# Layers and experts of a two-layer model in one block, with the first list's weights and rows prepared inside the layers' last turn

## The chip, the core and the metric

The kernel runs on one core of one Trainium2 chip, in one launch. The metric is the device time in microseconds. One execution is also profiled; its trace is what the prediction is worked out from.

## The reference, cut to what matters

The input is x of 2 x 2048 x 256. Layer 0 is a gated linear attention and a small per-feature network, layer 1 a selective scan (a state-space layer) and a mixture of experts. Each part takes a layer norm of x, scales and shifts it by a modulation vector, and adds its result to x with a gate. Only the last part matters closely here:

```python
k = int(EXPERT_CAPACITY * t / e)                   # 512 rows for each of 8 experts
scores = jnp.einsum('ntd,ed->nte', x, gate_w)
probs = jax.nn.softmax(scores, axis=-1)
g, m = jax.lax.top_k(probs.transpose(0, 2, 1), k)  # each expert chooses its rows
xin = x[batch_idx, m]
h = jnp.einsum('nekd,edf->nekf', xin, w1)          # 256 -> 1024
h = jax.nn.gelu(h, approximate=False)
h = jnp.einsum('nekf,efd->nekd', h, w2)            # 1024 -> 256
out = jnp.zeros((n, t, d)).at[batch_idx, m].add(g[..., None] * h)
```

All of it is float32. With 2 batch entries and 8 experts there are 16 lists of 512 rows.

## The kernel before

**The layers.** The 4096 rows are cut into 16 blocks (`NB`) of 256 rows. A software pipeline with stages A (attention), F (small network and the front of the scan), S and C (the scan and its back) and G (gate scores) runs in turns of 64 steps (`STEPS`). Turn i works on block i+2 in stage A, i+1 in F, i in S, i-1 in C, i-2 in G. The table `AT` gives each operation its step, and every engine walks the same steps in order and issues what is its own, with semaphores between engines. So the order on each engine is fixed in the program. In the scan, for each of 16 states m, ScalarE forms decays (L1143), TensorE turns them (L1113), GpSimd forms the input product (L1181), VectorE runs the recurrence (L1162), GpSimd multiplies by the readout (L1171), and TensorE adds these up in PSUM (L1130). Afterwards VectorE multiplies by a gate (`yz`, L1233), TensorE turns and projects (`yt` L1201, `out` L1209), VectorE adds to x (`x_scan`, L1239), ScalarE makes normalized rows that go to DRAM (`ln_d`, `rows_d`), and stage G turns and modulates them and forms scores (`turn_d` L567, `mod_d`, L1257).

**The choice of rows.** `Selection` finds each expert's 512 best rows for one batch entry in 21 steps (n = 0 to 20). A step is a few VectorE instructions (`dve_step`: three candidate thresholds and their counts), and between steps TensorE adds the counts over partitions (`pe_step`). Step 1 needs the exponentials from ScalarE (`act_exp`). Then for each list, `place` (VectorE, L300 and L304) makes one-hot matrices, `pe_slots` (L313) multiplies them, `slots` (L321, L322) reads the row numbers, and `gather` (GpSimd, L328, four indirect DMAs) fetches the rows. For batch entry 0 these steps stand in turns 15, 16 and 17 of the layers (`STEPS_AT`, `PLACES_AT`, `TURNS_AT`, `READS_AT`); for entry 1 they stand inside the lists (`IN_LIST`).

**The end of the layers.** Turns 17 (`NB + 1`, stages C and G) and 18 (G) close the pipeline. At its end GpSimd gathers lists 0 and 1, SyncE waits for the last stores, and the block ends with a barrier of all engines. The experts are a second block.

**The experts.** For each list TensorE turns the gathered rows (`turned`, tile `pt`, L1765), ScalarE modulates them (`rows_of`, L1730). For accuracy at speed each float32 operand is split into an upper part (ScalarE `put`, L1718) and a rest (VectorE `split`, L1665), and each product is three matmuls. The up-projection is 48 matmuls into `ph`, in 8 groups f; ScalarE applies the gelu (L1745), then `put` and `split`. The down-projection is 96 matmuls into `po`, in 4 groups s (both L1775); VectorE scales by the gates (L1702) and GpSimd adds the rows to the output by indirect DMA (L1825). The weights come over SyncE (`load_expert`, L338) into `w_in` in two halves, and are split in 8 pieces. Pieces of list k+1 are split during list k; those of list 0 are split after the barrier, with its rows (L1718, L1665), before the first up matmul.

Of the kernel before, what the change touches and what calls it, by code (L numbers as in the profile page):

```python
# [15 lines left out]
P = 128  # L16
# [134 lines left out]
class Selection:  # L151
# [30 lines left out]
    def act_exp(self, act, b):  # L182
        act.wait_ge(self.sem("centred"), b + 1)
# [150 lines left out]
def load_expert(sp, sem, k, w_in, w_ds):  # L334
    for n, (name, w_d) in enumerate(w_ds):
        if k >= 1:
            sp.wait_ge(sem("w_split"), (k - 1) * WQ + (n + 1) * WQ // 2)
        sp.dma_start(w_in[:, n * DC * F:(n + 1) * DC * F].rearrange("p (c f) -> p c f", c=w_d.shape[1] // P),  # L338
                     w_d[k % E:k % E + 1].rearrange("e (c p) f -> p (e c) f", p=P)).then_inc(sem(name), 16)


def build(nc, x_in, consts, weights, folds, wmod0, wmod1, w1_d, w2_d, out):
# [3 lines left out]
    with ExitStack() as top:  # L346
# [5 lines left out]
        def sem(name):  # L352
            if name not in names:
# [13 lines left out]
        layers(nc, sem, x_rows, consts, weights, folds, wmod0, wmod1, out_rows, xn_d,  # L367
               scores, fixed, ones_s, ident_s, col1, gb1, W, w_in, xg, select, w_ds)
        experts(nc, sem, select, w_ds, w_in, xg, out_rows, xn_d, ident_s, col1, gb1)


def layers(nc, sem, x_rows, consts, weights, folds, wmod0, wmod1, out_rows, xn_d,
           scores, fixed, ones_s, ident_s, col1, gb1, W, w_in, xg, select, w_ds):
    with ExitStack() as ctx:
# [17 lines left out]
        headones, upto_s, beyond_s, row64 = (fx(name) for name in ("headones", "upto", "beyond", "row64"))  # L392
        causal = sb("causal", [P, 4 * CH], mybir.dt.uint8)
        epst = sb("epst", [P, 1])
        ones_b = sb("ones_b", [P, P], BF16)
        wo_g = sb("wo_g", [P, B, DC, D])
        wout_g = sb("wout_g", [P, B, D])
        bout_g = sb("bout_g", [3 * 32, B, 2, D], BF16)
# [1026 lines left out]
        def turn_pe(pe, i, stages):  # L1425
# [5 lines left out]
            for n in range(STEPS):  # L1431
# [17 lines left out]
        def turn_act(act, i, stages):  # L1449
# [5 lines left out]
            for n in range(STEPS):  # L1455
# [18 lines left out]
        def turn_dve(dve, i, stages):  # L1474
            a, f, s, c, g = blocks_of(i, stages)
            for n in range(STEPS):
# [15 lines left out]
        def turn_pool(pool, i, stages):  # L1492
            a, f, s, c, g = blocks_of(i, stages)
            for n in range(STEPS):
                for it, m in ((c, n + STEPS), (s, n), (f, n - STEPS)):
                    if it is not None:
                        scan_pool(pool, it, m)

        def turn_sp(sp, i, stages):
# [25 lines left out]
            if i == NB - 1:  # L1525
                sp.wait_ge(sem("wo_mm"), NB + 1)
                sp.dma_start(select.consts, consts[:, FIXED_W:FIXED_W + EARLY_CONSTS]).then_inc(sem("const2_in"), 16)
# [16 lines left out]
            if i == NB:  # L1544
                load_expert(sp, sem, 0, w_in, w_ds)
            if f is not None:
                sp.wait_ge(sem("dkq"), f + 1)
                sp.dma_start(kq_d[bass.ds(f % 2, 1)].rearrange("o r t -> (o r) t"), dkq[P - 2 * DS:, :])\
                    .then_inc(sem("kq_out"), 16)
                sp.wait_ge(sem("ndt"), f + 1)  # L1550
# [5 lines left out]
        def pipeline(eng, a_turn):  # L1556
# [10 lines left out]
            a_turn(eng, NB + 1, "CG")  # L1567
            a_turn(eng, NB + 2, "G")

        with nc.Block() as block:  # L1570
            @block.sync
            def _(sp):
                sp.dma_start(fold[:, 0:2 * DC * B], folds[:, 0:2 * DC * B]).then_inc(sem("c_in"), 16)
                sp.dma_start(x_at(1, 0, NT).rearrange("p (t n) -> p t n", n=D),
                             x_rows[0:TB, :].rearrange("(t p) n -> p t n", p=P)).then_inc(sem("x_in"), 16)
                sp.dma_start(wmod[:, 0, :, 0:2 * D], wmod0.rearrange("(c p) n -> p c n", p=P)[:, :, 0:2 * D])\
                    .then_inc(sem("mod0_in"), 16)
                pipeline(sp, turn_sp)
                sp.wait_ge(sem("x_out"), (NB + 1) * 16)
                sp.wait_ge(sem("rows_out"), (NB + 1) * 16)  # L1580

            @block.tensor
            def _(pe):
                pe.wait_ge(sem("silc"), 2)
                pe.wait_ge(sem("mod0_in"), 16)
                mod_cols(pe, 0, MODS[0]).then_inc(sem("modcols"), 1)
                pe.wait_ge(sem("fixed_in"), 16)
                pipeline(pe, turn_pe)

            @block.scalar  # L1590
            def _(act):
                act.wait_ge(sem("c_in"), 16)
                for n in range(2):
                    act.activation(silc[:, n, :], fo(f"c{n}"), ACT.Silu).then_inc(sem("silc"), 1)
                act.preload_act_table_set("natural_log_exp_and_others")
                act.wait_ge(sem("tail0"), 2)
                pipeline(act, turn_act)

            @block.vector
            def _(dve):  # L1600

                dve.memset(epst[:, :], EPS)
# [300 lines left out]
```

## Time and profile before

| what | us |
| --- | --- |
| median of 3 runs | 1872.36 |
| the three runs | 1872.26, 1872.36, 1876.86 |
| the profiled execution | 1876.97 |
| its span | 1875.2 |
| TensorE busy (matmuls) | 1721.5 |
| VectorE busy | 1474.1 |
| GpSimd busy | 1376.4 |
| ScalarE busy | 1374.2 |

The span runs from the first instruction of the trace to the last. Busy times are of the whole span, whose stages have different limits: the layers fill it up to about 1450 us, the experts the rest. Times in rows are microseconds from the start of the span.

### The profile page before, as it was taken

The numbers are of one execution on the slowest core, as the hardware profiler recorded it, in microseconds if no ns is written. First come the engines' busy times: TensorE is split into PE (matmuls) and PEld (weight loads), VectorE is DVE, ScalarE is ACT, GpSimd is POOL, SyncE is SP. The second block draws the span as 40 slices with busy tenths as digits, with TensorE's granted clock in tenths as the row PEclk, the third lists the DMA queues.
The fourth block names the chain that finished last, engine by engine and source line by source line (L and its number), as shares of the span: only waits on it lengthen the run. The fifth ranks groups of instructions, "written<-read, shape, count | busy, mean of one in ns | idle before, by whom it ended". The sixth has DMA issues, their size and how long they took to land. (4 is left out here: it accounts for less than half of the span.)

```text
span 1875.2 us, 34292 instructions
## 1 busy us (share of the span) xinstructions
PE 1721.5 (92%) x12348; PEld 1486.3 (79%) x12348; DVE 1474.1 (79%) x3114; ACT 1374.2 (73%) x2701; POOL 1376.4 (73%) x644
## 2 busy tenths in 40 slices
PE   6689999999999999999999999997777799999997
PEld 5567788887978888787888878787666688899996
DVE  3557888888888888888888889888896687766663
ACT  3468888888888888889888888986642566566663
POOL 0009899898999989899998989999996245445442
PEclk9999999999999999999999999999887899999998
DMA  4012222223222322322233132213231344555552
GB/s 193 1 41 62 63 64 74 65 56 91 63 71 62 74 78 43 91 74 63 59 74 80 41 95 70 65 51 84 85 72 59 99 110 123 135 136 135 136 135 23
DMA packets 120888, 149.88 MB, mean 80 GB/s; under 512 B 8208, under 2 KB 111120, under 8 KB 120336
## 3 DMA queue, kind: packets, MB, share of 16 engines
q1 hardware_dynamic: 108432, 130.91, 25.5%
q0 software_dynamic: 12288, 16.79, 5.2%
q8 instruction: 98, 1.61, 0.4%
q14 instruction: 70, 0.57, 0.1%
HBM read 121.98 MB, written 17.30 MB: 74 GB/s over the span
## 5 line engine op out<-in xcount | busy, mean ns | idle before, releaser
L1181 POOL TENSOR_TENSOR room<-room 128x1024 f32<-128x1024 f32 x256 | 605.7, 2366 | 180.4 <-DVE room L1096 141.4
L1162 DVE TENSOR_TENSOR_SCAN room<-pD,last,room 128x256 f32<-128x256 f32 x1024 | 691.8, 733 | 50.9 <-PE pD L1113 38.6
L1171 POOL TENSOR_TENSOR room<-room 128x1024 f32<-128x1024 f32 x256 | 605.7, 2366 | 61.9 <-PE pY L1130 61.0
L1143 ACT ACTIVATE room<-room,fixed,kkT 128x512 f32<-128x512 f32 x512 | 406.5, 806 | 53.3 <-PE pD L1113 51.0
L1113 PE MATMUL pD<-fixed,room 128*128 128x128 f32 x2048 | 318.1, 279 | 49.1 <-DVE room L1162 47.4
L1130 PE MATMUL pY<-fixed,room 128*128 128x128 f32 x2048 | 319.7, 280 | 15.6 <-POOL room L1171 15.5
L1113 PEld LDWEIGHTS pD<-fixed,room 128*128 128x128 f32 x2048 | 243.2, 144 | 77.4 <-issue 44.4
L1130 PEld LDWEIGHTS pY<-fixed,room 128*128 128x128 f32 x2048 | 249.5, 146 | 67.2 <-POOL room L1171 31.4
L328 POOL DMA_INDIRECT xg<-xn_rows,W x64 | 68.5, 1071 | 202.4 <-DVE W L322 187.4
L1745 ACT ACTIVATE h<-ph 128x512 f32<-128x512 f32 x128 | 76.6, 599 | 140.7 <-PE ph L1775 110.8
L1825 POOL DMA_INDIRECT y_out<-ys,W x64 | 115.8, 1809 | 48.2 <-DVE ys L1702 29.3
L1775 PE MATMUL po<-w_up,h_up 128*128 128x256 f32 x512 | 148.7, 290 | 0.5 <-DVE h_rest L1665 0.5
L1775 PE MATMUL po<-w_rest,h_up 128*128 128x256 f32 x512 | 144.8, 283 | 0.0
L1775 PE MATMUL po<-w_up,h_rest 128*128 128x256 f32 x512 | 144.7, 283 | 0.0
L1665 DVE TENSOR_TENSOR h_rest<-h,h_up 128x512 fp32r<-128x512 f32 x128 | 85.1, 690 | 73.3 <-ACT h_up L1718 69.9
L712 PE MATMUL pA<-hA,W 128*128 128x256 f32 x512 | 121.0, 380 | 1.6 <-DVE w_in L801 1.6
L1775 PE MATMUL ph<-hg_up,w_up 128*128 128x512 f32 x256 | 101.7, 397 | 3.5 <-DVE hg_rest L1665 3.5
L712 PEld LDWEIGHTS pA<-hA,W 128*128 128x128 f32 x512 | 92.5, 190 | 12.4 <-DVE w_in L801 2.4
L1775 PE MATMUL ph<-hg_rest,w_up 128*128 128x512 f32 x256 | 100.8, 394 | 0.0
L1775 PE MATMUL ph<-hg_up,w_rest 128*128 128x512 f32 x256 | 100.5, 392 | 0.0
L1775 PEld LDWEIGHTS po<-w_up,h_up 128*128 128x128 f32 x512 | 98.0, 191 | 1.9 <-DVE h_rest L1665 1.8
L1775 PEld LDWEIGHTS po<-w_rest,h_up 128*128 128x128 f32 x512 | 98.2, 192 | 0.0
(307 smaller groups left out, 3580.1 us busy)
## 6 DMA issues: line engine op xcount, KB each, us to landing
room<-kq_rows SPq DMA_DIRECT2D x256, 256.0 KB, 5.4
w_in<-w_d SPq DMA_DIRECT2D x32, 1024.0 KB
room<-ndS SPq DMA_DIRECT2D x16, 512.0 KB, 3.3
xt<-x_in SPq DMA_DIRECT2D x16, 256.0 KB, 2.9
y_out<-xo SPq DMA_DIRECT2D x16, 256.0 KB, 2.1
xn_rows<-xnC SPq DMA_DIRECT2D x16, 256.0 KB, 2.1
W<-weights SPq DMA_DIRECT2D x1, 1808.0 KB, 9.2
W<-weights SPq DMA_DIRECT2D x1, 1697.5 KB, 16.7
```

Source lines behind the costliest of these rows:

```text
L328: pool.indirect_dma_start(xg[:, k % 2, s, :], None, xn_d[0:(k // E + 1) * T, :], bass.IndirectOffsetOnAxis(ap=self.ids[:, k * SL + s:k * S ...
L712: i = pe.matmul(bank[:, h2 * TB:(h2 + 1) * TB], wt[:, c, h * DK:(h + 1) * DK], hA[:, c, :], start=(c == 0), stop=(c == DC - 1))
L1113: i = pe.transpose(pD[h][:, k2 * TB + t * P:k2 * TB + (t + 1) * P], decT[:, m % 2, t, (2 * h + k2) * P:(2 * h + k2 + 1) * P], ident_s[:, :])
L1130: i = pe.matmul(pY[:, t, k * P:(k + 1) * P], sq[:, m % 2, k, t * P:(t + 1) * P], ident_s[:, :], start=False, stop=(m == DS - 1), is_transp ...
L1143: act.activation(decT[:, m % 2, t, :], turn2(ndT, it, NT * DI, t * DI, DI), ACT.Identity, bias=ones_s[:, 0:1], scale=turn2(kkT, it, NT * D ...
L1162: dve.tensor_tensor_scan(run, pD[h][:, k2 * TB:(k2 + 1) * TB], run, last[:, bass.ds(later(it) * (DS * DT) + m * DT + k, 1)], ALU.mult, ALU ...
L1171: pool.tensor_tensor(sq[:, m % 2], st[:, m % 4], kqb[:, m % SLOTS, 1, :].unsqueeze(1).broadcast_to([P, DT, TB]), ALU.mult).then_inc(sem("r ...
L1181: pool.tensor_tensor(st[:, m % 4], turn2(u, it, DT * TB).rearrange("p (k t) -> p k t", k=DT), kqb[:, m % SLOTS, 0, :].unsqueeze(1).broadca ...
L1665: dve.tensor_tensor(rest, whole, upper.bitcast(F32), ALU.subtract).then_inc(sem(done), 1)
L1745: act.activation(h1[:, f % 4, :], ph[:, f % 2, :], ACT.Gelu).then_inc(sem("gelu"), 1)
L1775: m = pe.matmul(to, stationary(c, p0), moving(c, p1), start=(c == 0 and n == 0), stop=(c == chunks - 1 and n == 2))
L1825: pool.indirect_dma_start(out_rows, bass.IndirectOffsetOnAxis(ap=select.ids[:, k * SL + s:k * SL + s + 1], axis=0), ys[:, k % 2, s, :], No ...
```

## The change

There is one block now. `layers` issues turns up to 16 and hands back functions for the rest; `experts` issues turns 17 and 18 in pieces between its own work. The allocations in SBUF and PSUM are laid out so that what list 0 needs early lies over what the layers have finished with. No computation is added or left out.

```diff
-        STEPS_AT = [(NB - 1, n) for n in (27, 36, 45, 51, 57)]
-        STEPS_AT += [(NB, n) for n in (3, 8, 14, 23, 28, 32, 36, 40, 44, 48, 52, 56)]
-        STEPS_AT += [(NB + 1, n) for n in (0, 4, 8, 12)]
-        PLACES_AT, TURNS_AT, READS_AT = ([(NB + 1, n) for n in at] for at in ((21, 23), (26, 29), (29, 31)))
+        STEPS_AT = [(NB - 1, n) for n in (17, 27, 29, 36, 52, 57, 63)]
+        STEPS_AT += [(NB, n) for n in (5, 9, 14, 22, 30, 35, 38, 45, 52, 56, 58, 62)]
+        STEPS_AT += [(NB + 1, n) for n in (0, 3)]
+        PLACES_AT = [(NB + 1, 13), (NB + 1, 13)]
+        TURNS_AT = [(NB + 1, 13), (NB + 1, 22)]
+        READS_AT = [(NB + 1, 13), (NB + 1, 25)]
```

The constants of the choice (`const2_in`) are loaded in turn 14 instead of 15. The gathers of lists 0 and 1 follow GpSimd's part of turn 17, each when its row numbers are there; there is no wait for the last stores. The order on the engines from turn 17 on:

```diff
+        IN_LIST = {(1 + n // 4, n % 4): n for n in range(SUMS + 2)}
+        YZ, YT, PUTS = AT["yz1"], AT["yt1"], 5
+        LN = AT["ln_d"]
+        TURN, SCORE = range(0, AT["turn_d"] - STEPS + 2), range(AT["turn_d"] - STEPS + 2, STEPS)
...
+            for half in range(2):
+                load_half(sp, sem, 1, half, w_in, w_ds)
+            last.sp(sp, NB + 1, "CG")
...
+            last.dve(dve, NB + 1, "CG", range(0, YZ + 1))
+            for q in range(WQ // 2):
+                split_weights(0, q, q + 1)
+            for c in range(DC):
+                split(hg[:, c, :], hg_up[:, c, :], hg_rest[:, c, :], "hg_split", WQ // 2 + c + 1)
+            last.dve(dve, NB + 1, "CG", range(YZ + 1, STEPS))
...
+            last.act(act, NB + 1, "CG", range(0, PUTS))
+            put_weights(0, 0)
+            last.act(act, NB + 1, "CG", range(PUTS, YT + 1))
+            rows_of(0)
+            last.act(act, NB + 1, "CG", range(YT + 1, LN))
+            act.preload_act_table_set("gelu_and_others")
+            for k in range(NL):
+                for f in range(FT):
...
+                    if k == 0 and 2 <= f < 2 + WQ // 2:
+                        put_piece(0, WQ // 2 + f - 2)
...
+                if k == 0:
+                    act.preload_act_table_set("natural_log_exp_and_others")
+                    last.act(act, NB + 1, "CG", range(LN, STEPS))
+                if k == 1:
+                    select.act_exp(act, 1)
+                if k + 1 < NL:
+                    rows_of(k + 1)
+                    put_weights(k + 1, 0)
+                    if k == 0:
+                        last.act(act, NB + 2, "G", TURN)
+                    put_weights(k + 1, 1)
+                    if k == 0:
+                        last.act(act, NB + 2, "G", SCORE)
...
+            last.pe(pe, NB + 1, "CG", range(0, YT + 1))
+            turned(0)
+            last.pe(pe, NB + 1, "CG", range(YT + 1, STEPS))
...
+                    if k == 0 and s in (1, 3):
+                        last.pe(pe, NB + 2, "G", TURN if s == 1 else SCORE)
```

`YZ` is 19, `YT` 22 and `LN` 40. So the projection `out` (step 25) and `x_scan` (28) come after list 0's rows are turned and before its first up matmul, the last block's norm after list 0's gelus, and its turn and scores inside list 0's down-projection. The second half of list 0's weights is split inside its up-projection (VectorE: one piece behind each of the splits f = 1 to 4). In list 0 `place` for list 2 follows f = 7 (before: f = 3), `pe_slots` follows s = 1 and `slots` s = 2. Entry 1's choice of rows takes no slot in list 0, and four in each of lists 1 to 5 (before: four in list 0 and three in each of lists 1 to 5).

## Rows read from the trace of the kernel before

**Rows 1.** The page's part 2, TensorE: busy tenths in 40 slices of 46.9 us

```profile
PE   6689999999999999999999999997777799999997
```

**Rows 2.** Chain that ended last, 1415 to 1475 us: start, us, what

```profile
1461.36 2.19 ACT w_up L1718 x4
...
1465.43 1.30 DVE hg_rest L1665 x2
...
1466.78 5.29 PE ph L1775 x12
```

**Rows 3.** Timeline, TensorE, 1416 to 1466: start, us, instruction, [idle before <-releaser]

```profile
1434.26 2.80 PE L1130 MATMUL pY<-fixed,room 128*128 128x128 f32 x12
...
1440.59 5.41 PE L1209 MATMUL pB<-oproj_g,xraw 128*128 128x256 f32 x16 [0.69 <-ACT xraw L1219]
...
1450.36 0.63 PE L567 MATMUL pB<-fixed,xnC 128*128 128x128 f32 x4 [1.61 <-ACT xnC L559]
1452.18 1.87 PE L1257 MATMUL pB<-W,xnA 128*128 128x8 f32 x8 [1.19 <-ACT xnA L576]
1461.38 1.94 PE L1765 MATMUL pt<-fixed,xg 128*128 128x128 f32 x8 [7.33 <-PEq L1570]
```

**Rows 4.** Timeline, GpSimd, 1344 to 1362 and 1416 to 1480

```profile
1354.89 2.35 POOL L1181 TENSOR_TENSOR room<-room 128x1024 f32<-128x1024 f32 x1
...
1432.19 2.35 POOL L1171 TENSOR_TENSOR room<-room 128x1024 f32<-128x1024 f32 x1 [0.93 <-PE pY L1130]
1448.95 1.14 POOL L328 DMA_INDIRECT xg<-xn_rows,W  x1 [14.40 <-DVE W L322]
...
1457.96 0.95 POOL L328 DMA_INDIRECT xg<-xn_rows,W  x1 [0.30 <-issue]
```

**Rows 5.** Stretches: from:to, length, busy of five engines, clock, DMA share, GB/s

```profile
1360.00:1420.00 60.00, 42.51 (x285) 35.55 (x285) 55.18 (x171) 26.40 (x54) 60.00 (x27) 0.89 0.34 88
...
1444.00:1446.00 2.00, 2.00 (x16) 1.64 (x15) 0.00 (x0) 0.00 (x0) 0.00 (x0) 0.91 0.00 0
...
1460.00:1461.00 1.00, 0.00 (x0) 0.00 (x0) 0.00 (x0) 0.00 (x0) 0.00 (x0) 0.50 0.13 45
...
1466.00:1471.50 5.50, 4.72 (x11) 3.80 (x12) 4.29 (x10) 4.38 (x8) 0.00 (x0) 0.50 0.51 187
```

**Rows 6.** Timeline, VectorE, 1344 to 1358 and 1416 to 1480

```profile
1353.23 1.26 DVE L1096 TENSOR_TENSOR room<-pB,xs 128x512 f32<-128x512 f32 x2
...
1427.40 2.66 DVE L1162 TENSOR_TENSOR_SCAN room<-pD,last,room 128x256 f32<-128x256 f32 x4
...
1436.30 1.49 DVE L1233 TENSOR_TENSOR tmpT<-pY,szT 128x512 f32<-128x512 f32 x2 [2.71 <-PE pY L1130]
...
1438.10 2.29 DVE L304 TENSOR_TENSOR W<-W 128x2048 bf16<-128x2048 f32 x1
```

**Rows 7.** Instructions of L1745: min/median/max ns, first and last start

```profile
L1745 ACT ACTIVATE h<-ph x128: 597/598/604, 1469.8 to 1849.8; 128x512 f32<-128x512 f32 x128
L1745 ACT ACT_TABLE_LOAD  x1: 1283/1283/1283, 1468.5 to 1468.5; - x1
```

**Rows 8.** Chain that ended last, 1495 to 1876 us

```profile
1495.73 2.75 PE ph L1775 x12
...
1502.81 0.85 issue
...
1521.89 4.12 PE ph L1775 x18
...
1527.87 0.14 DVE W L228
...
1529.56 0.39 PE pc L194 x2
...
1625.17 10.91 PE ph L1775 x48
...
1648.97 10.91 PE ph L1775 x48
```

More of the change, by code:

```diff
@@ L1 @@
+from collections import namedtuple
 from contextlib import ExitStack
@@ L366, in build, with layers @@
         w_ds = (("w1_in", w1_d), ("w2_in", w2_d))
[L367 to L372, printed above, removed]
+        with nc.Block() as block:
+            last = layers(nc, block, sem, x_rows, consts, weights, folds, wmod0, wmod1, out_rows, xn_d,
+                          scores, fixed, ones_s, ident_s, col1, gb1, W, w_in, xg, select, w_ds)
+            experts(nc, block, sem, select, last, w_ds, w_in, xg, out_rows, xn_d, ident_s, col1, gb1)
+LastTurns = namedtuple("LastTurns", "sp pe act dve pool")
+def layers(nc, block, sem, x_rows, consts, weights, folds, wmod0, wmod1, out_rows, xn_d,
            scores, fixed, ones_s, ident_s, col1, gb1, W, w_in, xg, select, w_ds):
@@ L1423, in blocks_of, with turn_pe @@
             return [i + d if s in stages else None for s, d in (("A", 2), ("F", 1), ("S", 0), ("C", -1), ("G", -2))]
-        def turn_pe(pe, i, stages):
+        def turn_pe(pe, i, stages, steps=range(STEPS)):
             a, f, s, c, g = blocks_of(i, stages)
@@ L1430, in turn_pe @@
                 pe.wait_ge(sem("early"), 1)
-            for n in range(STEPS):
+            for n in steps:
                 if i < 1:
@@ L1447, in turn_pe, with turn_act @@
                 choose_pe(pe, i, n)
-        def turn_act(act, i, stages):
+        def turn_act(act, i, stages, steps=range(STEPS)):
             a, f, s, c, g = blocks_of(i, stages)
@@ L1454, in turn_act @@
                 act.wait_ge(sem("early"), 1)
-            for n in range(STEPS):
+            for n in steps:
                 if i < 1:
@@ L1472, in turn_act, with turn_dve @@
                     select.act_exp(act, 0)
-        def turn_dve(dve, i, stages):
+        def turn_dve(dve, i, stages, steps=range(STEPS)):
             a, f, s, c, g = blocks_of(i, stages)
-            for n in range(STEPS):
+            for n in steps:
                 if i < 1:
@@ L1490, in turn_dve, with turn_pool @@
                 choose_dve(dve, i, n)
-        def turn_pool(pool, i, stages):
+        def turn_pool(pool, i, stages, steps=range(STEPS)):
             a, f, s, c, g = blocks_of(i, stages)
-            for n in range(STEPS):
+            for n in steps:
                 for it, m in ((c, n + STEPS), (s, n), (f, n - STEPS)):
@@ new lines, in _ @@
+        @block.tensor
+        def _(pe):
+            pe.wait_ge(sem("silc"), 2)
+            pe.wait_ge(sem("mod0_in"), 16)
+            mod_cols(pe, 0, MODS[0]).then_inc(sem("modcols"), 1)
+            pe.wait_ge(sem("fixed_in"), 16)
+            pipeline(pe, turn_pe)
+        @block.scalar
+        def _(act):
+            act.wait_ge(sem("c_in"), 16)
+            for n in range(2):
+                act.activation(silc[:, n, :], fo(f"c{n}"), ACT.Silu).then_inc(sem("silc"), 1)
+            act.preload_act_table_set("natural_log_exp_and_others")
+            act.wait_ge(sem("tail0"), 2)
+            pipeline(act, turn_act)
@@ L1624, in experts, with _ @@
+        @block.gpsimd
+        def _(pool):
+            for name, n in PER_BLOCK.items():
+                pool.sem_inc(sem(name), n)
+            pipeline(pool, turn_pool)
+        return LastTurns(turn_sp, turn_pe, turn_act, turn_dve, turn_pool)
+def experts(nc, block, sem, select, last, w_ds, w_in, xg, out_rows, xn_d, ident_s, col1, gb1):
     with ExitStack() as ctx:
@@ new lines, in piece, with _ @@
+            return w_in[:, n * DC * F + (q % 4) * h:n * DC * F + (q % 4 + 1) * h], w_up[slot][n][:, at], w_rest[slot][n][:, at]
+        IN_LIST = {(1 + n // 4, n % 4): n for n in range(SUMS + 2)}
+        YZ, YT, PUTS = AT["yz1"], AT["yt1"], 5
+        LN = AT["ln_d"]
+        TURN, SCORE = range(0, AT["turn_d"] - STEPS + 2), range(AT["turn_d"] - STEPS + 2, STEPS)
+        @block.sync
+        def _(sp):
+            for half in range(2):
+                load_half(sp, sem, 1, half, w_in, w_ds)
+            last.sp(sp, NB + 1, "CG")
+            for k in range(2, NL):
+                for half in range(2):
+                    load_half(sp, sem, k, half, w_in, w_ds)
```

442 lines of the change are left out of this document (208 added, 234 removed).

## The prediction

> **What bounds the kernel now.** I read the slices first: TensorE is at 6 in the first slice, at 9 for most of the run, and at 7 in five slices from about 1310 to 1540 us [rows 1]. The change is at about 1450, in this dip, so I read the chain of waits across it. The chain there is no data from the layers: at 1461.36 ScalarE starts to split list 0's weights, then rows are modulated, VectorE makes their rest (1465.43), and the first up matmul of the experts starts at 1466.78 [rows 2]. What held 1461.36 is in the timelines. TensorE finished the sums of the scan at 1437.06, projected until 1446.00, turned and scored the last block until 1454.05, and then waited 7.33 us, by the profile for its own sequencer: the barrier [rows 3]. GpSimd is the engine that came last to it. It made its last scan product at 1432.19 to 1434.54, stood 14.40 us waiting for list 0's row numbers, and issued eight gathers from 1448.95 to 1458.91 [rows 4]. The DMAs still moved 45 GB/s in the stretch 1460 to 1461 [rows 5]. So some 29 us pass between the last scan sum and the first up matmul, in which TensorE has about 12 us of work.
>
> Before that, GpSimd is the bound: from 1360 to 1420 it is busy 60.00 of 60 us, VectorE 55.18 [rows 5]. After it, TensorE is: a late list takes 1648.97 - 1625.17 = 23.80 us. Lists with steps of the choice take longer: 26.16 for list 1, and (1625.17 - 1495.73) / 5 = 25.9 on average for lists 1 to 5 [rows 8]. List 0 takes 1495.73 - 1466.78 = 28.95 [rows 2, 8]: its first 12 up matmuls take 5.29 us, 0.44 each, at a granted clock of 0.50 (1.2 GHz), where the late lists take 10.91 / 48 = 0.227 [rows 2, 5, 8]; the rest is VectorE's `place` and selection between the splits.
>
> **Part 1: when list 0 starts.** The last selection steps of entry 0 leave turn 17, so `place` for list 0 follows the last scan directly. The scan ends at 1430.06 [rows 6]; without the steps in front of it perhaps 0.7 earlier, since its input product is made by about 1426.7, one GpSimd instruction of 2.35 before each of the readouts. `place` takes about 2.7 (2.29 and a smaller instruction) [rows 6], so to 1432.1; `pe_slots` and `slots` to 1433. `place` for list 1 then fills VectorE to about 1436, before `yz` can start. TensorE now stands at step 13 until 1432.1 for the one-hot matrices. Behind it are the sums of states 14 and 15 and a block's scores; this puts their end at about 1438.0 where it was 1437.06: +0.9. `yz` and `yt` follow as before, and `yT` ends at about 1441.5 (before: 0.05 ahead of the projection at 1440.59 [rows 3]).
>
> GpSimd is free at about 1434.4 and has the row numbers. Gathers are issued every (1457.96 - 1448.95) / 7 = 1.29 us [rows 4], so list 0's four end at 1439.2. The last of eight ended its issue at 1458.91 and traffic was nearly gone at 1460 to 1461 [rows 4, 5], so landing takes 1.5 to 2 us: 1441. Both feed `turned(0)` at 1441.3. It takes 1.94 at the low clock [rows 3]: 1443.3. Then the projection, 5.41 for 16 matmuls [rows 3], to 1448.8. Beside it ScalarE and VectorE prepare the rows: from the end of `pt` (1463.32) to the first up matmul it took 3.46 us [rows 2, 3], so they are ready at 1446.8, under the projection. The weights' first half is split where ScalarE idles (2.19 us [rows 2]) and behind `yz` on VectorE (four of 0.65, to about 1441.3). If that cover were gone, the 2.19 and these 2.6 would stand on the path. Next late after the barrier is thus TensorE's own order: the projection that was put behind the rows.
>
> The low clock need not recur in list 0: it rose to 0.91 in the stretch 1444 to 1446, during the projection [rows 5], and now up matmuls follow it without a pause. Ends: no extra cost to the 2.4 us of the 12 slow matmuls; I take none.
>
> **Part 2: the layers' last turns.** Turns 15 and 16 get 19 selection steps instead of 17, two more by the end of turn 15. A step is VectorE from 1527.87 to 1529.52, 1.65 us [rows 8]. VectorE is idle 8% there, but not where it matters: GpSimd, which has no slack, starts block 16's first input product at 1354.89, and the `u` it needs ends at 1354.49 [rows 4, 6]. By then one more step has run. So the price is 1.65 - 0.40 = 1.25, less what VectorE's waits absorb. Ends: 0 (absorbed) and 3.3 (two full steps). I take 1.1, near the row. The constants' DMA merely moves a turn; 0. List 0 starts at 1448.8 + 1.1 = 1449.9: **-16.9**.
>
> **Part 3: list 0.** TensorE's work is 23.80, and now also the last block's turn and scores, 0.63 + 1.87 = 2.5 [rows 3]: 26.3. It loses its selection steps. ScalarE has four weight pieces more in the up phase, 0.55 each on top of a gelu of 0.60 and an upper part of about 0.55 [rows 2, 7]: 1.6 a group against TensorE's 1.36, four times, so it falls 0.9 behind, which two `ph` buffers roughly hold. VectorE's `place` stands behind the last split, no longer between splits. Ends 25.4 (turn and scores at the high clock) and 29 (as before, one of these covers failing); I take 26.3 against 28.95: **-2.6**.
>
> **Part 4: list 1.** Selection step 1 is at f = 5 on VectorE and needs `act_exp(1)`. ScalarE has that behind all eight gelus and their upper parts. VectorE therefore stands, with the splits of f = 6 and 7 queued behind, and TensorE's down-projection needs these. From the up phase's end at 10.9: gelu and two upper parts 1.7, table load 1.28, two small activations 0.6 (estimate), step 1.65, two splits 1.30 [rows 2, 7, 8]: 17.4. Undisturbed, TensorE would reach chunk 6 at 10.9 + 0.9 + 2.3 = 14.1 and finish the group at 15.0; now at 17.8, **2.8 late**. Against that, list 1 no longer has the stop at f = 4 (0.85) and the matmuls there (about 0.4) [rows 8], and slot 1 costs less. Ends: 0 and 5 late; net I take **+1.2** on 26.16.
>
> ScalarE now changes tables at list 0's end, for `act_exp(1)` and back, where one load stood [rows 7]. The Trainium skill, "ScalarE: Activation LUTs", What ACT_TABLE_LOAD costs, says that a switch is the load of 1283 ns plus a drain of about 1380 ns. The load agrees with the trace's 1283; no row here shows the drain. By it list 1 would be 1.4 later, and the total saving 16.0.
>
> **Part 5: lists 2 to 6.** The fourth slot in lists 2 to 5 adds a pair of small matmuls each (0.1) and list 5 gets full steps where it had light ones: **+0.9**. Later lists are unchanged; list 6's one step has VectorE's idle time.
>
> **Sum.** -16.9 - 2.6 + 1.2 + 0.9 = -17.4. Against the profiled execution's own 1876.97 this gives 1859.6. That execution lay with the upper of the three runs; against the median of 1872.36 it gives **1855.0**, my forecast.
>
> **Rivals.** (a) *The covers hold better*: no slip in the turns (-1.1), list 0 at 25.4 (-0.9), the choice's stop in list 1 absorbed (-2.8): 1872.4 - 22.2 = 1850. For it: VectorE has 4.8 us idle in 60 [rows 5]. Against: the `u` margin of 0.4. Chance 0.22.
> (b) *New waits eat half*: ScalarE becomes the bound of list 0 (29, +2.7), the slip is 3.3 (+2.2), the low clock recurs (+2.4), list 1 is 2 us worse: 1855 + 9.3 = 1864. For it: the clock was 0.50 at list 0's start [rows 5]. Chance 0.15.
> (c) *The split transition brings little*: the rows of list 0 land late, because `turned(0)` heads TensorE's queue and the projection, `x_scan` and everything else stand behind it. It would need some 12 us of delay to come within 0.3% of before. Against: GpSimd's 14.40 idle [rows 4]. About 1869. Chance 0.04.
> (d) *Slower*: VectorE becomes the bound of turns 15 to 17. Each step makes a round trip to TensorE, whose own queue then stops the decays that the scan needs; if each of 19 steps costs GpSimd 1.2 us instead of nothing, that is 23 us. It decides from 0.92 us a step (17.4 / 19). At 1.2: 1878. For it: VectorE at 92%. Against: GpSimd loses nothing with 17 steps now. Chance 0.04.
>
> **How the numbers follow.** The forecast has 0.55. A difference under 0.3% (5.6 us) can't be told from none here. (a), (b) and the forecast are all faster: 0.92. (c) and neighbours are the same: 0.04. (d) is slower: 0.04. The range goes from below (a)'s 1850, since its terms could each be an us better, to (b)'s 1864: 1847 to 1864.
>
> **What would show it.** The last scan product ends at 1434 to 1437, with a gather right behind. `pt` stands before the 16 matmuls of the projection; the first up matmul comes 0.1 us behind them at a granted clock near 1.00. List 0 lasts about 26, list 1 shows VectorE waiting for the exponentials and TensorE for the splits. Wrong would be: idle GpSimd between 1280 and 1430 of over 3 us, a wait in front of `pt` of over 3 us, or a list 0 over 29.

## The result

The changed kernel takes 1870.26 us (median of 18 runs, 1866.60 to 1873.40) beside 1876.11 for the kernel before on the same chip (18 runs, 1872.10 to 1878.61). The ratio is 0.9972, with an interval of 0.9965 to 0.9978. The change gains 5.9 us between the medians (0.31%), and 0.28% by the ratio. The interval excludes 1, but the size lies at the 0.3% below which the forecast called two times the same. It is a third of the 17.4 forecast, and 1870.26 is outside the range of 1847 to 1864. The forecast counted from 1872.36, a median of three runs; over 18 runs the kernel before has 1876.11. So of the 15.3 us between 1855.0 and 1870.26 some 11.5 are gain that did not come, and 3.8 are the starting point.

The profiled execution took 1872.29, with a span of 1870.5 (before: 1875.2). In its slices TensorE's dip at the transition is shorter than in [rows 1]: 8, 8, 7 and 6 where five stood at 7. (The forecast put those five at 1310 to 1540 us; by slices of 46.9 us they are 1266 to 1500.)

```profile
PE   6688999999999999999999999998876999999997
```

The transition is read on three engines. First TensorE, the answer to [rows 3]: start, us, instruction, and in brackets the idle time before it with what ended it.

```profile
1440.67 0.60 PE L315 MATMUL pA<-W 128*128 128x20 bf16 x16 [5.63 <-DVE W L306]
...
1443.58 2.80 PE L1136 MATMUL pY<-fixed,room 128*128 128x128 f32 x12
...
1451.00 1.97 PE L1809 MATMUL pt<-fixed,xg 128*128 128x128 f32 x8 [0.44 <-DMA xg<-xn_rows,W]
1452.77 5.27 PE L1215 MATMUL pB<-oproj_g,xraw 128*128 128x256 f32 x16
1457.68 0.58 PE L1819 MATMUL ph<-hg_up,w_up 128*128 128x512 f32 x1
```

The first up matmul starts at 1457.68 where it was 1466.78. It follows the projection with no pause, as forecast. But TensorE stands 5.63 us at step 13, waiting for VectorE's one-hot matrices (L306). VectorE's timeline, the answer to [rows 6], says why:

```profile
1431.24 2.67 DVE L1168 TENSOR_TENSOR_SCAN room<-pD,last,room 128x256 f32<-128x256 f32 x4 [0.78 <-PE pD L1119]
1433.84 4.58 DVE L302 TENSOR_TENSOR W<-W 128x320 bf16<-128x320 bf16 x1
1438.34 2.28 DVE L306 TENSOR_TENSOR W<-W 128x2048 bf16<-128x2048 f32 x1
...
1441.47 0.48 DVE L302 TENSOR_TENSOR W<-W 128x320 bf16<-128x320 bf16 x1
```

The first instruction of `place` takes 4.58 us for list 0 and 0.48 for list 1: the same line, the same shape. The long one ends 0.36 us behind GpSimd's last scan product, as GpSimd's timeline shows (the answer to [rows 4]); 1431.12 + 6.94 is 1438.06:

```profile
1431.12 6.94 POOL L1177 TENSOR_TENSOR room<-room 128x1024 f32<-128x1024 f32 x3
1442.44 2.73 POOL L330 DMA_INDIRECT xg<-xn_rows,W  x1 [4.38 <-DVE W L324]
1445.48 0.98 POOL L330 DMA_INDIRECT xg<-xn_rows,W  x1 [0.30 <-issue]
```

GpSimd then waits 4.38 us for the row numbers, and its first gather takes 2.73 us where the next takes 0.98. VectorE's L306 for list 1, from 1441.87 to 1444.16, lies beside it.

Two more losses lie elsewhere. The table of stretches (from:to, length, busy of five engines, clock, DMA share, GB/s) gives block 16's first readout product to the last readout's start, and the first up matmuls. The first is 142.28 us; before it was 1432.19 - 1291.68 = 140.51. The second has the high clock, 1.00, where [rows 5] had 0.50:

```profile
1293.45:1435.73 142.28, 105.71 (x661) 89.60 (x659) 128.37 (x347) 73.90 (x150) 139.18 (x61) 0.88 0.27 72
...
1457.68:1463.00 5.32, 5.32 (x24) 4.30 (x23) 2.39 (x6) 2.45 (x5) 2.50 (x3) 1.00 0.34 99
```

The waits of GpSimd between 1293 and 1376 (engine, line, what for: total, times, longest) name the places of that slip. Before, the only one of note was 0.5 us on `pY`.

```profile
POOL room L1187 <- DMA room<-kq_rows: 1.7, 1, 1.7
POOL room L1177 <- PE pY L1136: 1.4, 1, 1.4
```

In the experts, the chain of waits (start, us, what) shows list 1. It starts at 1483.90 and ends at 1512.39, 28.49 us where [rows 8] had 26.16; between its phases the chain goes through the exponentials and the selection. (Where lengths of lists are compared below, they run in the timeline from one list's first up matmul to the next one's; that gives 28.47 here and differs from the chain by up to 0.2.)

```profile
1483.90 11.27 PE ph L1819 x48
...
1497.14 1.28 ACT L188
...
1499.83 0.29 DVE W L260
1500.13 0.61 DVE h_rest L1686
...
1500.78 1.65 PE po L1819 x6
1502.43 0.44 PE pc L315 x16
...
1512.39 2.79 PE ph L1819 x12
```

The same list in the kernel before, where the up phase ends (1508.28) and where the first group of the down-projection ends (1512.31):

```profile
1508.28 0.87 PE pt L1765 x8
...
1512.31 0.41 PE pc L313 x16
```

And something that I had called unchanged is not: the late lists. Two of them in the same chain:

```profile
1642.45 11.14 PE ph L1819 x48
...
1666.49 11.19 PE ph L1819 x48
```

Their 48 up matmuls take 11.14 and 11.19 us where [rows 8] has 10.91, and lists 7 to 14 last 24.03 and 23.89 in turn, where all were 23.80.

**Where the time went.** The start-up before GpSimd's first readout product differs from execution to execution, by up to 3.7 us between the kernels run here; that product starts at 149.58 before and at 151.34 after. From there to the first up matmul the changed kernel is 10.86 us shorter. List 0 is 2.7 shorter, list 1 2.3 longer, lists 2 to 6 3.0 longer, lists 7 to 15 with the tail 1.8 longer. Together -6.5, less the 1.8 of start-up: -4.7, the difference of the spans.

### The profile page after: what moved, and what is told of

Its sections match the earlier page's. It is cut to its first block, busy times and chain, and to the rows that moved or that the text cites. A ratio compares the mean times of both kernels' runs of the same rounds, so it can differ in the third digit from the quotient of the medians.

```text
span 1870.5 us, 34289 instructions
## 1 busy us (share of the span) xinstructions
PE 1724.7 (92%) x12348; PEld 1486.4 (79%) x12348; DVE 1477.8 (79%) x3114; ACT 1379.2 (74%) x2705; POOL 1371.7 (73%) x644
## 4 chain that ended last, share of the span: by engine, by line
PE 76%; POOL 7%; DVE 6%; issue 6%; ACT 3%; DMA 0%; POOLq 0%; DVEq 0%; ACTq 0%
PE po L1819 9%; PE pY L1136 9%; PE pD L1119 9%; PE ph L1819 9%; PE pA L718 6%; POOL room L1177 3%; PE pA L620 3%; PE pB L915 3%; DVE room L1168 3%; PE pB L925 3%; POOL room L1187 3%; PE pB L1215 3%; PE pB L946 2%; PE pA L646 2%; PE pA L611 2%
## 5 line engine op out<-in xcount | busy, mean ns | idle before, releaser
L1136 PE MATMUL pY<-fixed,room 128*128 128x128 f32 x2048 | 319.2, 280 | 15.9 <-POOL room L1177 15.9
L1875 POOL DMA_INDIRECT y_out<-ys,W x64 | 109.5, 1710 | 48.4 <-DVE ys L1727 29.5
```

The source lines that it names most:

```text
L1136: i = pe.matmul(pY[:, t, k * P:(k + 1) * P], sq[:, m % 2, k, t * P:(t + 1) * P], ident_s[:, :], start=False, stop=(m == DS - 1), is_transp ...
L1875: pool.indirect_dma_start(out_rows, bass.IndirectOffsetOnAxis(ap=select.ids[:, k * SL + s:k * SL + s + 1], axis=0), ys[:, k % 2, s, :], No ...
```

## The experiments

The theory after the result was: VectorE's `place` is shut out by GpSimd's scan products while these run, and the gathers by VectorE's `place`. Rivals were a wait on data or slots, and the new positions of the selection's steps. Below, "start" is the stretch from GpSimd's first readout product, in the first turns, to the first up matmul, which leaves the start-up out: 1317.20 before, 1306.34 in the changed kernel.

**`a_swap`: the two instructions of `place` in the other order.**

```diff
+        dve.tensor_tensor(self.onehot[:, k % 2], iota..., lo..., ALU.is_equal)
         dve.tensor_tensor(entries..., quarter..., ALU.mult)
-        dve.tensor_tensor(self.onehot[:, k % 2], iota..., lo..., ALU.is_equal)
```

> The changed kernel, with the two instructions of every `place` in the other order: the one-hot compare first (float32 in, 128x2048, 2.3 us), the product of bfloat16 operands (128x320) second. Theory: VectorE's all-bfloat16 product cannot run while GpSimd's tensor products run, and in list 0 it stood 4.58 us until GpSimd was through at 1438.06. Then the compare runs in 2.3 us beside GpSimd, the product ends 0.3 to 0.5 us after GpSimd's last product, and the row numbers of list 0 come about 2 us earlier than in the changed kernel relative to that last product (3.4 us behind its end there, about 1.3 here). Time 1.5 to 2.5 us less than the changed kernel's 1870.3: about 1868.3. Rival: whichever instruction of the first `place` comes first is slow (code fetched late, or a wait that the trace doesn't show); then the compare takes some 6 us and nothing is gained, 1870.3.

Measured: 1868.80 us, ratio to before 0.9962 [0.9951, 0.9974]. VectorE's and GpSimd's timelines:

```profile
1431.61 6.38 DVE L302 TENSOR_TENSOR W<-W 128x2048 bf16<-128x2048 f32 x1
1437.91 0.48 DVE L304 TENSOR_TENSOR W<-W 128x320 bf16<-128x320 bf16 x1
```

```profile
1428.83 7.01 POOL L1177 TENSOR_TENSOR room<-room 128x1024 f32<-128x1024 f32 x3
1440.22 2.33 POOL L330 DMA_INDIRECT xg<-xn_rows,W  x1 [4.38 <-DVE W L324]
```

The wait goes with whichever instruction is first. The comparison, 2.28 us elsewhere, takes 6.38: until GpSimd's end at 1435.84, and then its own time. The small one behind it takes its 0.48. So the theory as it was written down, that only the small bfloat16 product is shut out, was wrong, and no data or slot of the small one is what was waited for. The start is 1304.75, 1.6 less than in the changed kernel, though the wait for the row numbers is the same 4.38: the first gather takes 0.4 less, and the projection 4.09 us instead of 5.27, at a granted clock of 0.87 from 1450.0 to 1453.7, where the changed kernel had 0.50 from 1452.7 to 1456.

**`b_late`: `place` for list 1 six groups later.**

```diff
-        PLACES_AT = [(NB + 1, 13), (NB + 1, 13)]
+        PLACES_AT = [(NB + 1, 13), (NB + 1, 19)]
```

> The changed kernel with `place` for list 1 moved from step 13 to step 19 of turn 17, behind the gate product. Theory: GpSimd's first gather instruction took 2.73 us instead of 0.96 because VectorE's `place` for list 1 ran beside it; with VectorE idle it takes 0.95 to 1.15, the four gathers of list 0 end 1.7 us earlier, and list 0's first up matmul starts 1 to 1.7 us earlier relative to GpSimd's last product (19.6 us behind its end in the changed kernel). Time about 1869. Rival: the first gather is slow by itself (in the kernel before it took 1.14, so not by much) and still takes over 2.5 us: 1870.3.

Measured: 1868.56, ratio 0.9962 [0.9949, 0.9975]. VectorE, GpSimd and a gather each wait in turn here. GpSimd paused between 1433.84 and 1434.55:

```profile
1431.91 2.28 DVE L302 TENSOR_TENSOR W<-W 128x320 bf16<-128x320 bf16 x1
1434.11 2.28 DVE L306 TENSOR_TENSOR W<-W 128x2048 bf16<-128x2048 f32 x1
...
1441.94 2.28 DVE L306 TENSOR_TENSOR W<-W 128x2048 bf16<-128x2048 f32 x1
```

```profile
1434.55 4.05 POOL L1177 TENSOR_TENSOR room<-room 128x1024 f32<-128x1024 f32 x1 [0.72 <-PE pY L1136]
1438.77 1.14 POOL L330 DMA_INDIRECT xg<-xn_rows,W  x1 [0.17 <-issue]
...
1442.76 2.29 POOL L330 DMA_INDIRECT xg<-xn_rows,W  x1 [0.31 <-issue]
```

`L306` was first this time, and GpSimd's product behind it takes 4.05 us instead of 2.35, 1.7 more; `L306` ends at 1436.39, 1.84 behind that product's start. That `L306` came first is not the edit's doing, since it did so in `d_exp` too, whose transition is the changed kernel's. The first gather is fast now (1.14), as expected, and the fourth, beside the moved `L306`, takes 2.29. From GpSimd's end to the first up matmul it takes 15.0 us instead of 19.6, but that end is itself put off by the 1.7: start 1303.31. And list 1 takes 29.93 instead of 28.47: behind its stall TensorE's granted clock was 0.50 from 1497 to 1503, and the 48 down matmuls took 7.59 us instead of 6.12.

**`c_steps`: the selection's steps as evenly as in the kernel before, the last at group 12 of the last turn.**

```diff
-        STEPS_AT = [(NB - 1, n) for n in (17, 27, 29, 36, 52, 57, 63)]
-        STEPS_AT += [(NB, n) for n in (5, 9, 14, 22, 30, 35, 38, 45, 52, 56, 58, 62)]
-        STEPS_AT += [(NB + 1, n) for n in (0, 3)]
+        STEPS_AT = [(NB - 1, n) for n in (27, 36, 45, 51, 57)]
+        STEPS_AT += [(NB, n) for n in (3, 8, 14, 23, 28, 32, 36, 40, 44, 48, 52, 56)]
+        STEPS_AT += [(NB + 1, n) for n in (0, 4, 8, 12)]
```

> The changed kernel with the selection steps of entry 0 where they were before the change (5 in turn 15, 12 in turn 16, and 0, 4, 8, 12 in turn 17); place, slots and gathers stay where the change puts them. Theory: the two steps more in turn 15 cost GpSimd's chain 2.7 us (its products ran 1.77 us behind the kernel before at the turn's start and 4.45 at its end); here the lag at the end of turn 16 is within 0.5 us of that at the start of turn 15. `place` for list 0 however starts after step 12 of turn 17, some 3 us later behind GpSimd's last product. Net within 1 us of the changed kernel, 1869.5 to 1871.5. Rival: the 2.7 us come from something else in the last turns (the constants' DMA in turn 14, for one); then the lag is still 2.5 to 3 and the time 1872 to 1873.

Measured: 1867.37, ratio 0.9957 [0.9942, 0.9972]. The stretch that had slipped, and `place`:

```profile
1293.63:1433.44 139.81, 104.50 (x659) 87.74 (x657) 126.06 (x348) 73.96 (x150) 138.95 (x61) 0.88 0.29 74
```

```profile
1434.91 1.29 DVE L302 TENSOR_TENSOR W<-W 128x320 bf16<-128x320 bf16 x1
```

The stretch takes 139.81 us instead of 142.28, 2.5 less between these two executions. The other traces bear it out, with a smaller mean: the five kernels with the changed positions take 141.30 to 142.28 us, the eight with the steps spread 139.58 to 140.51. `place` starts later, at 1434.91, and still waits until GpSimd's end (1435.85) and 0.35 more. The start is 1303.57. The time is below the 1869.5 to 1871.5 expected.

**`g_psum`: one operand of `place` read from PSUM.** ScalarE copies the ramp and the quarters there, eight groups into the last turn, for lists 0 and 1.

```diff
-    def place(self, dve, k):
+    def place(self, dve, k, bank=None):
+        if bank is not None:
+            dve.wait_ge(self.sem("in_bank"), 1)
+            iota, quarter = bank[:, a:a + P], bank[...]
...
+                if (i, n) == (NB + 1, 8):
+                    select.act_bank(act, pA[0])
```

> The changed kernel, where the place of lists 0 and 1 takes the ramp and the quarters from PSUM (copied there by ScalarE eight groups into the last turn), so that each of its VectorE instructions has one operand in SBUF and one in PSUM. Theory (VectorE and GpSimd shut each other out when VectorE reads two SBUF operands and GpSimd reads SBUF): the first place product takes about 0.5 to 0.7 us instead of 4.58, the compare about 2.3, both beside GpSimd's readout products, which keep their 2.31 to 2.35 each; the first gather takes 0.95 to 1.15 us instead of 2.73; list 0's first matmul comes 4 to 6 us earlier than in the changed kernel (1457.68). Rival (what delays the first place instruction is a wait on data or a slot, not the port): it still takes over 4 us, and the first gather over 2.2 us, and the time stays within 1 us of the changed kernel.

Measured: 1864.87, ratio 0.9945 [0.9927, 0.9962]. VectorE, then GpSimd:

```profile
1431.62 0.46 DVE L308 TENSOR_TENSOR W<-W,pA 128x320 bf16<-128x320 bf16 x1
1431.99 2.29 DVE L312 TENSOR_TENSOR W<-pA,W 128x2048 bf16<-128x2048 f32 x1
```

```profile
1428.65 7.05 POOL L1190 TENSOR_TENSOR room<-room 128x1024 f32<-128x1024 f32 x3
1436.05 1.15 POOL L343 DMA_INDIRECT xg<-xn_rows,W  x1 [0.35 <-issue]
```

Both instructions run in full beside GpSimd's products, and neither side is longer. The gather follows 0.35 us behind the last product. From GpSimd's end to the first up matmul it takes 1449.53 - 1435.70 = 13.8 us; in the changed kernel it was 1457.68 - 1438.06 = 19.6. The start is 1299.79, 6.55 less than in the changed kernel. The gain is a little over the expected 4 to 6. This settles the cause: where the operands lie decides, and apart from ScalarE's two copies and the semaphores for them nothing else was moved.

**`d_exp`: list 1's exponentials and first step at the end of list 0.**

```diff
+                if k == 0:
+                    select_step(0)
...
-                if k == 1:
-                    select.act_exp(act, 1)
...
                         last.act(act, NB + 2, "G", SCORE)
+                        select.act_exp(act, 1)
```

> The changed kernel with the first step of the selection for list 1's entry moved: its scores come at the end of list 0 and ScalarE's exp right behind them, before list 1 begins, in place of the stretch between list 1's two phases. Theory (the stall of list 1 is VectorE's chain behind that exp, some 2.3 us of 28.47): list 1 takes 25.6 to 26.2 us instead of 28.47, list 2 26.0 to 27.1, the whole 2.5 to 4 us below the changed kernel, ratio to the kernel before 0.995 to 0.9965 instead of 0.9972 by the earlier pairing. Rival (the stall only moves: the exp's table load now comes at the end of list 0, and TensorE waits there for h_up, ys or the table): list 0 grows by 1.5 to 2.5 us, list 1 shrinks by as much, and the total stays within 1 us of the changed kernel.

Measured: 1866.70, ratio 0.9953 [0.9936, 0.9969]. The chain has no ScalarE between list 1's phases any more:

```profile
1492.11 4.18 PE ph L1820 x18
1496.29 0.88 PE pt L1810 x8
1497.16 3.08 PE po L1820 x24
```

List 1 takes 26.44 instead of 28.47, list 2 26.44 instead of 27.10, list 6 23.89 instead of 24.46, and list 0 keeps its 26.1. All lists and the tail together take 409.29 us instead of 412.82. The 3.5 us are within the expectation, though list 1 itself stayed 0.25 above it: its stop at f = 4 is back.

The transition of this kernel is the changed kernel's, instruction for instruction, and it went otherwise. VectorE's and GpSimd's timelines, TensorE's, and the chain:

```profile
1434.40 2.28 DVE L306 TENSOR_TENSOR W<-W 128x2048 bf16<-128x2048 f32 x1
```

```profile
1434.84 4.04 POOL L1177 TENSOR_TENSOR room<-room 128x1024 f32<-128x1024 f32 x1 [0.71 <-PE pY L1136]
```

```profile
1450.48 1.97 PE L1810 MATMUL pt<-fixed,xg 128*128 128x128 f32 x8 [5.33 <-DMA xg<-xn_rows,W]
```

```profile
1444.37 6.06 DMA xg<-xn_rows,W
```

`L306` got in at a pause of GpSimd, as in `b_late`, so the gathers could start at 1439.05. But list 0's rows landed 6.06 us after the last gather began, where the changed kernel has 2.93, and TensorE stood 5.33 us for them; the start is 1306.47, no better than the changed kernel's. SyncE had issued the load of list 1's weights (1024 KB) at 1445.07, 0.7 us behind that gather; in the changed kernel it came 1.5 us behind. The DMAs moved 242 GB/s from 1446 to 1448 and 348 from 1448 to 1450. That this load held the rows back is a guess; no run moved it.

**`e_psum`: the kernel before with the banks of PSUM in the changed order**, for the late lists.

```diff
+        po = ps("po", [P, 2, 512])
         pc = ps("pc", [P, 2, 512])
...
-        po = ps("po", [P, 2, 512])
```

> The kernel before with only the experts' PSUM tiles in the changed kernel's order (po in the first two banks, then pc, pt, ph). In the changed kernel the lists 7 to 14 take 24.03 and 23.89 us in turn, and their 48 up matmuls 11.31 to 11.36, where the kernel before has 23.80 and 11.07. Theory A: the PSUM banks do it; then lists take about 23.96 on average here. Theory B: the place of the operands in SBUF does it; then 23.80 here. Over all lists it is worth some 2 us.

Measured: 1876.12 us in one run; lists 7 to 14 at 23.80. The banks are not it. (The expectation's 11.31 and 11.07 run to the end of the last matmul; the chain's 11.14 and 10.91 for the same ones run to where the next work starts.)

**`e_sbuf`: the kernel before with its buffers in SBUF placed as in the changed one.**

```diff
-        w_up = sb("w_up", [P, 2, 2, DC * F], F32R)
-        w_rest = sb("w_rest", [P, 2, 2, DC * F], F32R)
+        w_rest[0][1], w_up[1][0], w_rest[1][0] = weights_of("w2_rest0"), weights_of("w1_up1"), weights_of("w1_rest1")
+        still_used(1384)
...
```

> The kernel before, with the experts' buffers placed in SBUF in the order that the changed kernel gives them; instructions and their order are as before. Theory (the up matmuls of the late lists are slower in the changed kernel because of where the weights and rows lie in SBUF): lists 7 to 14 take 24.03 and 23.89 in turn instead of 23.80, and their 48 up matmuls 11.31 to 11.36 us instead of 11.07; the whole grows by 1.5 to 2.5 us. Rival (it is the order of DMA issues and loads between the phases): the lists stay at 23.80 and the up matmuls at 11.07.

Measured: 1876.88 in one run. The instructions are those of the kernel before, and the chain of two late lists is that of the changed one, to the hundredth:

```profile
1647.35 11.14 PE ph L1786 x48
...
1671.39 11.19 PE ph L1786 x48
```

Lists 7 to 14 take 23.89 and 24.03. From the first up matmul to the end it is 1875.09 - 1464.96 = 410.1 us against 408.4: 1.7 of the changed kernel's loss comes with the addresses.

**`i_hg` and `j_all`: 672 unused floats ahead of the moving rows (and the buffers behind them), and ahead of weights and rows together**, both in the kernel before.

```diff
+        sb("pad", [P, 672])
         hg = sb("hg", [P, DC, K])
```

> The kernel before with 672 unused floats (2688 bytes) of each partition ahead of hg, so that hg_up and hg_rest, the moving operands of the up matmuls, lie at the same place within 8 KB as in the changed kernel, while the weights stay. Theory (the place of the moving rows in SBUF sets the pitch of the up matmuls, 227 ns in the kernel before against 233 ns in the changed one): lists 7 to 14 take 23.9 to 24.05 us instead of 23.80. Rival (it is the place of the weights): they stay at 23.80.

> The kernel before with the same 672 floats ahead of the weights, so that weights and rows move together and keep their distances. Theory (the place within SBUF counts by itself): lists 7 to 14 take 23.9 to 24.05 us. Rival one (only the distance between weights and rows counts): 23.80. If this kernel is slower and the one with only the rows moved is not, it is the place of the weights.

Measured, one run each: 1874.19 and 1874.64. The chain of late lists, first with the rows moved, then with everything moved:

```profile
1644.98 11.16 PE ph L1776 x48
```

```profile
1646.57 10.91 PE ph L1776 x48
```

Lists 7 to 14 take 23.92 in the first and 23.80 in the second. It is not where the rows or the weights lie, but how far they lie from each other.

**`h_best`: three mends together** (the steps spread with the last at group 8 of the last turn, one operand in PSUM, the early exponentials).

```diff
+        STEPS_AT = [(NB - 1, n) for n in (27, 36, 45, 51, 57)]
+        STEPS_AT += [(NB, n) for n in (3, 8, 14, 22, 28, 32, 36, 40, 44, 48, 52, 56, 60)]
+        STEPS_AT += [(NB + 1, n) for n in (0, 4, 8)]
```

> The changed kernel with three mends together: the selection's steps spread evenly with the last at group 8 of the last turn, the place of lists 0 and 1 reading one operand from PSUM (copied at group 10), and list 1's exp at the end of list 0. If each answers to its own loss, they add: 3 us from the steps, 4 to 6 at list 0's start, 2.5 to 4 in list 1, in all 8 to 12 us below the changed kernel, so 1858 to 1862 us, ratio to the kernel before 0.990 to 0.993. Rival (all of them shift waiting to one place, GpSimd's last readout products, which set the end of the layers): no more than 4 us, 1866 to 1868.

Measured: 1860.12, ratio 0.9926 [0.9913, 0.9940]. The time is in the expected range, but one of its three terms is nothing. The PSUM operand and the early exponentials add; the spread steps do not: the stretch is 139.75 us instead of `g_psum`'s 141.30, but `place` starts only 2.7 us before GpSimd's end (there 4.1), TensorE holds the last sums back at step 13, and the first up matmul comes 15.8 us behind GpSimd's end instead of 13.8. The start, 1300.02, is no better than `g_psum`'s 1299.79.

**`k_pads`: the same with gaps that keep the distances modulo 512 bytes.**

```diff
-        still_used(1384)
+        still_used(1, 1408)
...
-        still_used(1336)
+        still_used(2, 1408)
...
-        still_used(1416)
+        still_used(3, 1320)
```

> The version with the three mends (steps spread, one operand of the place in PSUM, list 1's exp at the end of list 0), and the gaps between the experts' buffers changed from 1384, 1336 and 1416 floats to 1408, 1408 and 1320, so that slot 0's weights and the moving rows keep the kernel before's distance from slot 1's weights modulo 512 bytes. Theory (the distance between weights and moving rows sets the pitch of the up matmuls, and only within 512 bytes): pitch 227 ns instead of 232 to 233, lists 7 to 14 at 23.7 to 23.85 us instead of 24.03 and 23.89, the whole 1.5 to 2.5 us below that version (span 1857.1), ratio to the kernel before 0.991 to 0.992. Rival (a larger stretch than 512 bytes decides): lists stay at 23.9 to 24.05.

Measured: 1859.56, ratio 0.9916 [0.9902, 0.9931]; 15.9 us faster than the kernel before, and the best version. The lists are as they were:

```profile
1654.57 10.94 PE ph L1837 x48
```

Lists 7 to 14 take 23.82 and 23.80, and from the first up matmul to the end it takes 407.57 us instead of 409.45. The medians, taken on two chips, differ by only 0.6 of these 1.9 us, and the intervals overlap; the whole time does not show the rest.

## Why the prediction was wrong

**Part 1**, the start of list 0, is the step that failed: "`place` takes about 2.7 (2.29 and a smaller instruction) [rows 6], so to 1432.1". I took both durations from a row where GpSimd stood still [rows 4, 6] and laid them beside GpSimd's products. They do not run beside these: `place` ends 2.6 us behind GpSimd's last product instead of 2.3 ahead of it, and the gathers wait for it. The gather that was to stand right behind the last product came 4.38 us later. Counted from GpSimd's end, in us:

| | forecast | measured |
|---|---|---|
| to the first gather | 0 | 4.38 |
| four gathers issued | 4.8 | 6.7 |
| landed, `pt` starts | 2.1 | 1.9 |
| `pt`, projection, first up matmul | 7.5 | 6.7 |
| together | 14.4 | 19.6 |

With one operand in PSUM it is 13.8. The rest of the working held then; the clock at list 0's start (1.00) and the order rows, projection, up matmul were as forecast.

The kernel before is not fixed here either, which I overlooked. From GpSimd's end to the first up matmul its trace has 32.2 us and `e_psum`'s 32.4, but those of `e_sbuf`, `i_hg` and `j_all`, whose layers are the same, have 29.3 to 29.5. The 16 matmuls of the projection took 5.41 and 6.72 us in the first two, where the granted clock was 0.50 for part of the time, and 3.72 at 1.00 in the other three, as here in `i_hg`:

```profile
1438.04 3.72 PE L1209 MATMUL pB<-oproj_g,xraw 128*128 128x256 f32 x16 [0.69 <-ACT xraw L1219]
```

So up to 2.9 of the 10.86 us by which the start is shorter lie in the clock of the one execution compared against. The changed kernel's projection, 5.27 us, had 0.50 until 1456; by the same rows some 1.5 us (an estimate, 5.27 less 3.72) could still come off there.

The row that I lacked is no row of the trace before: no VectorE instruction with both inputs in SBUF lies beside a scan product anywhere in it. A rule would have pointed to it. The Trainium skill, "SBUF — State Buffer", Who interferes with whom, says that a VectorE instruction with two inputs in SBUF and a GpSimd instruction that reads SBUF shut each other out for a whole instruction, whichever starts first. By that rule, the traces agree: the 4.58, 6.38 and 4.05 us hold 4.1, 4.1 and 1.7 us of waiting, and with a PSUM operand there is none. The same section infers that such an instruction leaves the issue of GpSimd's own DMAs alone. For these gathers the measurement decides otherwise. Five that began inside the comparison took 2.73 (twice), 2.33, 2.29 and 1.73 us and ended 0.8 to 1.0 us behind it. In the lists, gathers that begin inside one of VectorE's splits (0.69 us, both inputs in SBUF) take up to 1.49 us (once 1.66), in the kernel before up to 1.46, and all others 0.94 to 1.15. So this half could have been read before. Whether the writing of the DMAs or the reading of the row numbers is what waits was not separated.

**Part 2**, the slip, was forecast at 1.1 and measured 1.8 beside the kernel before, 2.5 beside evenly spread steps. The sign was right and the place wrong: not the margin of `u` at 1354, but 1.7 us on the rows from DRAM at 1328 and 1.4 on the sums of the scan at 1341. The first can't be laid to the steps alone: `e_sbuf` and `k_pads`, whose steps are spread, wait 1.3 us for such rows too. One of my signs of being wrong came with this, GpSimd idle for 3.4 us between 1280 and 1430 (before: 0.65), though the slip is the smaller part of the miss.

**Part 3**, list 0: -2.6 forecast, -2.7 measured. **Part 4**, list 1: +1.2 forecast, +2.3 measured. The mechanism is the one described, exponentials, step and splits in front of the down-projection, and undoing it gave 3.5 us over all lists. The stop at f = 4 that I set against it did go: the up phase takes 11.27 us where it took 1508.28 - 1495.73 = 12.55. But the first group of the down-projection ends 18.5 us into the list (1502.43) where it ended at 16.6 (1512.31). So the stall is 3.2 us where I had 2.8, the rest of the list takes 0.4 more instead of less, and the granted clock was 0.50 from 1501 to 1503. With the same instructions in this list `c_steps` has 27.49 us at a clock of 1.00 from 1495 to 1507, `a_swap` 28.99 and `b_late` 29.93: part of the excess goes with the clock. The drain that the Trainium skill, "ScalarE: Activation LUTs", What ACT_TABLE_LOAD costs, adds to a load doesn't show here: ScalarE's next instruction starts 0.02 us behind the load's 1.28 (1497.14 + 1.28 = 1498.42, next at 1498.44), and the one ahead ends where the load starts. **Part 5**, lists 2 to 6: +0.9 forecast, +3.0 measured, of which 1.5 goes with the exponentials (`d_exp`) and 0.5 with the addresses (`e_sbuf`). "Later lists are unchanged" was wrong by 1.8: I read instructions and their order, not the addresses that the diff also changes.

**The sum.** -17.4 forecast. Part 1's shut-out 5.2 less, the slip 0.7, GpSimd's end taken 0.1 too early in the forecast, list 1 1.1, lists 2 to 6 2.1, late lists 1.8: -6.4 (-6.5 with list 0's 0.1), beside 5.9 us between the medians.

**The rivals.** None named this mechanism, and (a) was on the wrong side. (c) put the time right, 1869, and the place nearly: what stands behind list 0's rows did start late. But the rows waited 4.38 us for their numbers, not the 12 us of landing that it asked for; a late landing came only in `d_exp`, with 5.33 us. (b) had the right kind, several new waits, and took its 9.3 us from others: in all of list 0 TensorE stood 0.50 us, at a clock of 1.00. (d) is excluded by the changed kernel itself: its 19 steps cost 1.8 us, not 23.

**What stays open.** Why the distance between weights and rows counts isn't known. `k_pads` fits a period of 512 bytes and one of 256; 128 is out, since `i_hg`'s 2688 bytes are 21 times 128 and still changed the pitch. The slip went when the steps were moved (`c_steps`), but it was not traced to one of them. Why the rows landed late in `d_exp`, and which of the two orders of `L306` and the last scan product comes up in an execution, was not tested; each kernel has one trace.

## What to carry to other kernels

Before laying a VectorE instruction beside GpSimd's work, look where its operands lie: two in SBUF mean that one of the engines stands, and a stream of GpSimd products back to back keeps it out to the end; one operand in PSUM costs a copy and takes the collision away. A duration read where the neighbour engine was idle is the price there, not in the new place. A diff that moves buffers is a change of its own: compare a late, untouched stretch of both traces first, before giving differences to the edit.

## What the hardware showed that I had not expected

A waiting VectorE instruction does not get in between GpSimd's products when these follow each other without a gap: in the changed kernel and in `a_swap` it was ready within a product and waited for the rest of it and the whole next one, to the end of the row. In `b_late` and `d_exp`, with a gap of 0.7 us behind the product, it got in there.

Matmuls with the same instructions and shapes take 232 to 233 ns instead of 227 (11.14 and 11.19 us against 10.91 for 48) when only the distance between their weights and their moving rows in SBUF is different. The down matmuls of `i_hg` went the other way: 2.84 and 8.64 us where `j_all` has 2.87 and 8.74, so a list loses 0.12 and not 0.24.
